# First attention of a decoder: projection part 6 ahead of the second turning of the queries, the output product in two tiles, the division signalled per tile

## What is computed

```
q_in = x @ Wq.T + b;  Q = [q_in, conv3(q_in)] @ qproj.T      (keys the same way)
V = x @ Wv.T + b
tau, delta = sigmoid(gelu(depthwise conv3(x)) @ small matrices)
scores = Q K^T / sqrt(16) * tau + delta                     (16 heads of 16)
x = x + (softmax(scores) V) @ out_w.T + out_b
```

## Time and profile before

| what | value |
|---|---|
| median of 3 runs | 2564.86 us (2560.75 to 2569.78) |
| profiled execution | 2563.12 us, its span 2561.2 us |
| mean granted TensorE clock | 0.921 of full speed |
| TensorE matmul busy | 2154.4 us, 84% of the span |
| VectorE busy | 1573.9 us, 61% |
| ScalarE busy | 1221.2 us, 48% |
| GpSimd busy | 1052.0 us, 41% |
| first attention, TensorE's first to last product | about 54 to 599 us |
| of it, 13 like halves | 132.60 to 533.47 us |

### The profile page before, as it was taken

How to read it: one execution, slowest core, us unless ns; L and a number is a source line. 1 busy time by engine, 2 the same in 40 slices (tenths; PEclk the granted TensorE clock), 3 DMA queues, 4 the chain that set the end, 5 groups by cost and what they waited for, 6 DMA issues and landing times. The chain is left out here.

```text
span 2561.2 us, 45780 instructions
## 1 busy us (share of the span) xinstructions
PE 2154.4 (84%) x16918; PEld 1522.0 (59%) x16918; DVE 1573.9 (61%) x3193; ACT 1221.2 (48%) x1956; POOL 1052.0 (41%) x1204
## 2 busy tenths in 40 slices
PE   7699999986676379975999979984499999999996
PEld 5465666654555258863666658872276767666674
DVE  5477777775887746543777754557555555454552
ACT  2366666643111155543555543324446565564742
POOL 3987777720000033206555412210355555454533
PEclk8799999997878689997999998996699999999998
DMA  5000000000000233301111000003245444444422
GB/s 212 1 2 1 0 0 0 0 1 8 5 5 2 66 140 124 137 27 42 28 27 26 10 6 16 15 8 129 103 102 103 100 98 102 95 88 109 84 66 33
DMA packets 62562, 135.95 MB, mean 53 GB/s; under 512 B 10688, under 2 KB 46736, under 8 KB 55568
## 3 DMA queue, kind: packets, MB, share of 16 engines
q0 software_dynamic: 30976, 52.45, 10.1%
q1 hardware_dynamic: 31504, 82.41, 9.2%
HBM read 100.22 MB, written 34.60 MB: 53 GB/s over the span
## 5 line engine op out<-in xcount | busy, mean ns | idle before, releaser
L3036 ACT ACTIVATE f_h<-bank,f_b 128x512 f32<-128x512 f32 x256 | 175.9, 687 | 280.1 <-PE bank L176 272.8
L176 PE MATMUL ring<-f_w2hi,f_hidhi 128*128 128x256 f16 x1024 | 279.2, 273 | 6.1 <-DVE f_hidlo L3073 3.8
L3073 DVE TENSOR_TENSOR f_hidlo<-f_h,f_hidhi 128x512 f16<-128x512 f32 x256 | 177.3, 693 | 172.6 <-ACT f_hidhi L3037 172.6
L176 PE MATMUL ring<-f_w2hi,f_hidlo 128*128 128x256 f16 x1024 | 279.1, 273 | 0.0
L176 PE MATMUL ring<-f_w2lo,f_hidhi 128*128 128x256 f16 x1024 | 279.1, 273 | 0.0
L3127 POOL DMA_INDIRECT out<-f_y,f_to_row x128 | 211.9, 1656 | 47.6 <-issue 34.1
L176 PE MATMUL bank<-f_xthi,f_w1hi 128*128 128x512 f16 x512 | 194.9, 381 | 4.9 <-DVE f_w1lo L3056 4.9
L176 PE MATMUL bank<-f_xtlo,f_w1hi 128*128 128x512 f16 x512 | 194.8, 380 | 0.0
L176 PE MATMUL bank<-f_xthi,f_w1lo 128*128 128x512 f16 x512 | 194.8, 380 | 0.0
L1869 POOL COPY c_from_row<-c_token 128x5 uint32 (+1 forms) x8 | 1.5, 184 | 424.3 <-POOLq L1592 345.7
L3037 ACT ACTIVATE f_hidhi<-bank,f_b 128x512 f16<-128x512 f32 x256 | 173.9, 679 | 0.0
(11 more groups left out here) (537 smaller groups left out, 5899.1 us busy)
## 6 DMA issues: line engine op xcount, KB each, us to landing
f_raw<-in_e_w SPq DMA_DIRECT2D x32, 1024.0 KB
c_raw<-in_e_w SPq DMA_DIRECT2D x16, 1024.0 KB, 5.8
slots_out<-c_y POOLq DMA_DIRECT2D x8, 640.0 KB, 3.7
x<-in_x SPq DMA_DIRECT2D x1, 4096.0 KB
tokens<-c_xn SPq DMA_DIRECT2D x16, 256.0 KB, 2.4
tokens<-f_xn SPq DMA_DIRECT2D x16, 256.0 KB, 2.4
out<-x SPq DMA_DIRECT2D x1, 4096.0 KB, 14.3
wb<-in_wb SPq DMA_DIRECT2D x1, 3096.0 KB, 31.8
```

The costliest lines, as they stand in the source:

```text
L176: mm = pe.matmul(out, left[a], right[b], start=first and n == 0, stop=last and n == 2)
L3036: act.activation(h32[n % 4][:, :], src, ACT.Gelu_apprx_tanh, bias=bias).then_inc(sig["h_full"], 1)
L3073: dve.tensor_tensor(hid_v[1][:, it, at], h32[n % 4][:, :], hid_v[0][:, it, at], ALU.subtract).then_inc(sig["h_lo"], 1)
```

## The change

- TensorE: the second `rows` step stands ahead of `turn_weighed` and `turn_x`, no longer behind them. Projection part 6 stands ahead of `turn_again`. `output` makes one tile a call: tile 0 behind `columns_of_scores` 0, tile 1 behind `columns_of_scores` 2.
- VectorE: the division signals each tile by itself (`on_ready0`, `on_ready1`) in place of one signal behind both. Projection part 0 waits for tile 0, part 4 for tile 1; `turn_o` for both.
- ScalarE: exponential 1 stands ahead of `high_queries`, no longer behind it.

No instruction is added or taken away, but for the waits. `divide_by_sums` isn't called any more; its work stands in `divide`.

```diff
--- before.py
+++ after.py
@@ -640,7 +640,8 @@
                     side, t, part = n // 4, n // 2 % 2, n % 2
                     if n == 0:
                         pe.wait_ge(u["x_parts_ready"], i.now)
-                        pe.wait_ge(u["on_ready"], i.before)
+                    if n % 4 == 0:
+                        pe.wait_ge(u[f"on_ready{side}"], i.before)
                     bk = u.ring_bank[side]
                     for m in range(3 * part, 3 * part + 3):
                         k, h = divmod(m, KT)
@@ -720,7 +721,8 @@
                         pe.wait_ge(w["q_ready"], j.now)
                         pe.wait_ge(w["k_ready"], j.now)
                     elif c == 1:
-                        pe.wait_ge(other(u)["on_ready"], w_before.now)
+                        for t in range(NT):
+                            pe.wait_ge(other(u)[f"on_ready{t}"], w_before.now)
                     if c >= 2:
                         pe.wait_ge(u["exp_done"], i.count(8, c - 1))
                     for kt in range(NT):
@@ -759,19 +761,21 @@
                         mm.then_inc(u[f"o_made{t}"], 1)
 
                 def turn_o(u, i, x_turned):
-                    pe.wait_ge(u["on_ready"], i.now)
+                    for t in range(NT):
+                        pe.wait_ge(u[f"on_ready{t}"], i.now)
                     if x_turned:
                         pe.wait_ge(other(u)["x_pad_ready"], x_turned.now)
                     transpose_entry(pe, mem, u.low, u.on[:, :]).then_inc(u["on_transposed"], 1)
 
-                def output(u, i):
-                    pe.wait_ge(u["on_t_copied"], i.now)
-                    for t in range(NT):
-                        for h in range(KT):
-                            pe.matmul(u.high[:, t * D:(t + 1) * D], u.on_t_v[:, h, t * P:(t + 1) * P],
-                                      w_o[:, h, :], start=h == 0, stop=False)
-                        mm = bias(u.high[:, t * D:(t + 1) * D], 1)
-                    mm.then_inc(u["out_made"], 1)
+                def output(u, i, t):
+                    if t == 0:
+                        pe.wait_ge(u["on_t_copied"], i.now)
+                    for h in range(KT):
+                        pe.matmul(u.high[:, t * D:(t + 1) * D], u.on_t_v[:, h, t * P:(t + 1) * P],
+                                  w_o[:, h, :], start=h == 0, stop=False)
+                    mm = bias(u.high[:, t * D:(t + 1) * D], 1)
+                    if t == NT - 1:
+                        mm.then_inc(u["out_made"], 1)
 
                 def front(w, j, v):
                     turn_x(w, j, None)
@@ -789,11 +793,11 @@
                 def half(u, i, w, j, w_before, v):
 
                     rows(u, i, 0, w_before)
+                    rows(u, i, 1, w_before)
                     if w_before:
                         turn_weighed(other(u), w_before)
                     if v:
                         turn_x(u, v, w_before)
-                    rows(u, i, 1, w_before)
                     rows(u, i, 2, w_before)
                     if w:
                         project_qk(w, j, 0)
@@ -816,15 +820,18 @@
                         project_qk(w, j, 4)
                         sum_tau_delta(w, j)
                         project_qk(w, j, 5)
+                        project_qk(w, j, 6)
                     turn_again(u, i)
                     if w:
-                        project_qk(w, j, 6)
                         project_qk(w, j, 7)
                     columns_of_scores(u, i, w, j, w_before, 0)
                     if w_before:
-                        output(other(u), w_before)
-                    for c in (1, 2, 3):
+                        output(other(u), w_before, 0)
+                    for c in (1, 2):
                         columns_of_scores(u, i, w, j, w_before, c)
+                    if w_before:
+                        output(other(u), w_before, 1)
+                    columns_of_scores(u, i, w, j, w_before, 3)
                     weigh(u, i, 0)
                     if w:
                         turn_queries(w, j, 1)
@@ -846,7 +853,8 @@
                 last = stagger_ahead(pe, twins, front, half)
                 turn_weighed(twins[1], last)
                 turn_o(twins[1], last, None)
-                output(twins[1], last)
+                for t in range(NT):
+                    output(twins[1], last, t)
 
             @block.scalar
             def _(act):
@@ -940,10 +948,11 @@
                         copy_td_parts(w, j)
                         exp_td(w, j)
                     copy_again(u, i)
-                    exponentials(u, i, 0)
+                    for c in range(2):
+                        exponentials(u, i, c)
                     if w:
                         high_queries(w, j)
-                    for c in range(1, 5):
+                    for c in range(2, 5):
                         exponentials(u, i, c)
                     if w:
                         copy_v(w, j)
@@ -1108,7 +1117,15 @@
                     dve.tensor_copy(u.o_t_v[:, g, :], u.o_bank[g % 2][:, 0:S]).then_inc(u[f"o_t_ready{g}"], 1)
 
                 def divide(u, i):
-                    divide_by_sums(dve, u, i.now, order, u.ring_bank, u.rec, u.on)
+                    for t in range(NT):
+                        o = u.ring_bank[t].rearrange("p (h c) -> p h c", c=32)
+                        r = u.rec[:, t * H:(t + 1) * H]
+                        dve.wait_ge(u[f"o_made{t}"], i.now)
+                        order.step(dve.reciprocal(r, o[:, :, DH]))
+                        order.wait()
+                        dve.tensor_tensor(heads(tiles(u.on[:, :])[:, t, :]), o[:, :, 0:DH],
+                                          r.unsqueeze(2).to_broadcast([P, H, DH]), ALU.mult
+                                          ).then_inc(u[f"on_ready{t}"], 1)
 
                 def update(u, i):
                     residual_add(dve, sig, mem, i.before * 2 + u.p, i.now, u["out_made"], u.high, None, order, None
```

## The result

| | before | changed |
|---|---|---|
| median of 4 runs | 2566.41 us (2560.75 to 2569.78) | 2549.76 us (2547.82 to 2553.08) |
| ratio | | 0.9939, 95% interval 0.9917 to 0.9961 |
| profiled execution, span | 2563.12, 2561.2 us | 2547.82, 2545.8 us |

A forecast was written before the change was run, and what follows sets the result against it. TensorE's order was taken to bound each steady half, only its 2.70 us of waits being winnable. Thirteen halves at 29.97 gave -11.3 us; +1.0, -0.1 and -1.2 made -11.6: 2551.5 profiled, stated as 2553, range 2542 to 2563.

The forecast's parts named there:

- Rows and division: Early TensorE steps of a half: projection 0 at 2.47 us, 0.61 earlier; eighth maximum at 10.15 instead of 10.59.
- Cast and subtraction: VectorE before `turn_again`: cast goes ahead of GpSimd's addition, ending near 11.80 us; subtraction is held until 13.20 instead of 14.54.
- Rival A: VectorE's subtraction slips through unheld: half 29.47 us, -18 us in all, or 2547; chance 0.28.
- Part 6: Projection part 6 ahead of `turn_again`: 0.98 us of products fill the old 1.16 us wait and cost nothing; `turn_again` at 13.82.
- the first step of the same text: Rows order and split division put VectorE 0.44 us ahead, so its cast is issued before GpSimd's addition.
- Output and exponential 1: Later part of the half: old 0.90 us wait filled; columns 1 at 18.06, `stack_queries` 0.41 later at 20.52, `project_v` at 22.80.
- Rival C: GpSimd blocks VectorE's `stack_keys` and `low_x`; one absorbed, each further costs 1.3 us a half: +23 or 2588; chance 0.08.
- Uneven halves: First attention's halves outside the 13 alike: +1.0 us for half 0, -0.1 without convolution, -1.2 for the last.
- Half 0: First half, no division: part 6 in front delays the chain; bounds 0 and 1.96 us, taken as +1.0.
- Without convolution: The half in which GpSimd has no convolution: -0.1 us.
- The last: Last half, no projection: exponentials start earlier with one output tile moved behind columns 2; bounds 0 and -1.9 us, taken as -1.2.
- Total: Whole kernel: -11.3 us over the 13 halves, -11.6 in all, to 2551.5 by the profiled execution, stated as 2553.

The follow-up runs named there:

- e3: Kernel before with only the second `rows` moved and the division split: 29.59 us a half, 2546.0 us in total.
- e4: Changed kernel with the second `rows` behind `turn_x` again and projection part 0 waiting for both division tiles: 30.36 us a half, 2559.1 us in total.
- e6: Kernel before with GpSimd's two additions of convolution part 1 held until VectorE's subtraction of the maxima is done: 29.63 us a half, 2550.1 us in total.
- e7: Kernel before with only projection part 6 moved ahead of `turn_again`: 30.12 us a half, 2554.0 us in total.
- e2: Changed kernel with projection part 6 behind `turn_again` again: 29.90 us a half, 2551.7 us in total.
- e8: Kernel before with only output tile 1 moved behind columns 2: 30.30 us a half, 2560.1 us in total.
- e5: Kernel before with only exponential 1 moved ahead of `high_queries`: 31.91 us a half, 2580.8 us in total.
- e1: Changed kernel with `high_queries` ahead of exponential 1 again: 28.94 us a half, median 2538.7 us, ratio 0.9902 to the kernel before.

## Why the prediction was right, and where not

- **Rows and division:** right. `turn_weighed` stayed, projection 0 came at 2.47 as worked out, the eighth maximum at 10.13 (forecast 10.15). e3 and e4 show that these two parts together move the cast.
- **Cast and subtraction:** right in both. The cast took 0.17 more than its free 0.24, as the last short step of GpSimd was still running; the subtraction, issued 0.06 us behind GpSimd's addition, was held as long as forecast. The page "SBUF — State Buffer" of the Trainium skill (Who interferes with whom) says that a VectorE instruction with two SBUF inputs contends with a GpSimd instruction that reads SBUF, under an exclusive lock of the port pair. The trace agrees: the subtraction has two SBUF inputs and took 1.38 us beside the addition and 0.30 us in e6, where none ran. Rival A didn't come. It was less open than the forecast took it: the earlier trace rows hold the same case already, the subtraction at 330.14, 0.06 us behind the second addition at 330.08, and 1.36 us long. The start 0.02 behind that wasn't held was beside a short `tensor_scalar`, not an addition.
- **Part 6:** its cost of nothing was right, its use was overrated. The text said that it fills the old wait of 1.16. But the first step of the same text had taken that wait away, down to 0.4 (e3), and behind it VectorE's chain up to `take_k` sets columns 1. e7 shows the 0.71 that the old wait gives, e2 the zero that is left.
- **Output and exponential 1:** the arithmetic was right (measured against forecast: columns 1 at 17.87 for 18.06, `stack_queries` 20.34 for 20.52, `project_v` 22.69 for 22.80), the account was not. The step that failed is the sentence that output tile 1 and the exponential fill the old 0.90 wait. The tile does: with it the wait is 0.2 (e8), without it the whole 0.9 stands (e3). The exponential's move alone left it at 0.9 (e5), and its price, `stack_queries` later, was seen in the sum but not set against leaving the exponential where it was. Taken out, it gives 0.97 a half. The total came out as forecast all the same, because the sum carried that price.
- **Rival C:** its blocks came, two of them, 1.30 and 1.39 us, and cost next to nothing: from `project_v` to the next half it took 7.20 us, where 7.17 was forecast. The text had the second block cost 1.3 a half, with a reserve of 0.9. The reserve was larger: before the change VectorE stood idle 1.43 us before `take_weighed` 1 and 0.42 before `copy_queries` 0 (343.80 and 344.65 us), 1.85 in all. The two steps are 2.09 us longer than before, of which `low_x` behind them gives back 0.26 (0.73 for 0.99), and the first step of `stack_keys` 0.22 (0.68 for 0.90).
- **Uneven halves:** three mis-sized terms. Half 0: +1.0 forecast, +0.06 measured. `turn_again` does come 1.66 later there (117.83 for 116.17) and columns 1 waits 1.01 for `take_k`, but TensorE's granted clock is back at 1.00 when `turn_again` starts (1.06 us for it, where it took 1.79), and the fourth columns, which had waited 1.46 for an exponential, wait 0.90. Without convolution: -0.1, measured -0.30. The last: -1.2, measured +0.14. There the exponentials do start earlier, but TensorE's granted clock was lower in the 8.5 us behind `turn_again` (0.50 for 0.56):

```profile
574.50:583.00 8.50, 7.04 (x38) 4.76 (x38) 1.45 (x3) 2.50 (x3) 0.00 (x0) 0.56 0.00 0
...
562.20:570.70 8.50, 7.34 (x37) 4.84 (x38) 0.69 (x1) 3.98 (x4) 0.00 (x0) 0.50 0.00 0
```

Windows of the kernel before, then of the changed one. In e1, whose last half has the same order, the clock was 0.60 in the 8.5 us behind `turn_again`, output tile 1 took 1.13 us where it takes 2.08 in the changed kernel, and the half was 1.25 shorter (32.38 from the first `rows` to the last product's end), which is -1.1 against the kernel before. So the forecast's -1.2 is near where the clock rises earlier; why it did in e1 is open.
- **Total:** -11.3 for the 13 halves (measured -12.1), -11.6 in all (-12.2). The 0.8 is 0.06 a half: `take_k` came 0.18 earlier than worked out (17.04 for 17.22), `project_v` 0.11. That -12.2 is so close to -11.6 is in part luck, as the terms of the uneven halves missed by -0.9, -0.2 and +1.3. What the medians show beyond 12.2 us lies outside the changed part.

## What to carry over

Where a tiny step of one engine is long in the trace, look at what its neighbour does at that moment, and cost it at its free length from a stretch in which the neighbour is idle; whether it meets the neighbour can turn on tenths of a microsecond that are moved far away. The waits of one engine aren't a list from which each edit wins its own: price each edit with the others in place and without them. And of a change in several parts, work out the half without each part: here one part took back about half of what the others give (0.97 of the 1.90 us a half that e1 wins over the kernel before).

## What was not expected of the hardware

A small step of VectorE was held up for the whole length of a GpSimd addition that began only 0.06 us earlier (1.38 us for a step of 0.30), and even 0.03 us earlier (e4, 1.34 us for a step of 0.24), while one that started together with the addition was not (0.24 us), nor one 0.02 us behind a short step. GpSimd's additions stayed 1.26 to 1.28 us beside the waiting steps of `stack_maxima`, but one was stretched to 1.81 us itself where a two-input step of VectorE, the first of `stack_keys`, began at nearly the same time (334.55 and 334.56 us in the changed kernel) and took 0.68. That an additional wait on GpSimd makes a kernel 1.2 us a half faster without any work taken away is this, seen from the other side.
